# A selective-scan stage in which GpSimd weighs two neighbouring state tiles per operation

## The reference, cut to what matters

```
xc, z = split(x @ in_w.T);  xc = silu(conv(xc));  dt, B, C = split(xc @ x_w.T);  dt = softplus(...)
h[t, d, s] = exp(dt * A[d, s]) * h[t-1, d, s] + dt * B[t, s] * xc[t, d]      # 16 states s
y[t, d]    = sum over s of h[t, d, s] * C[t, s]  +  xc[t, d] * D[d]
out        = (y * silu(z)) @ out_w.T
```

## Time and profile before

| | before |
|---|---|
| median of three runs | 966.7 us |
| the profiled execution's own time | 964.93 us |
| its span | 963.1 us |
| TensorE matmul busy | 790.4 us, 82% of the span |
| VectorE busy | 704.1 us, 73% |
| GpSimd busy | 515.5 us, 54% |
| ScalarE busy | 369.9 us, 38% |

### The profile page before, as it was taken

One profiled execution on the slowest core, in us unless ns is written; L12 is line 12 of the kernel. 1 busy time (PEld: TensorE's weight loads), 2 busy tenths in 40 slices (PEclk: granted clock), 3 DMA queues, 4 the chain that ended last, 5 costly groups with the idle time before them and its releaser, 6 DMA issues. The chain is left out here.

```text
span 963.1 us, 18898 instructions
## 1 busy us (share of the span) xinstructions
PE 790.4 (82%) x7645; PEld 487.0 (51%) x7657; DVE 704.1 (73%) x911; ACT 369.9 (38%) x557; POOL 515.5 (54%) x403
## 2 busy tenths in 40 slices
PE   8888888889998757878877887878887887788696
PEld 4555554556664534545554555545554545455464
DVE  4985985550004018999999999999999898975798
ACT  1220002123333575455555555455655454321000
POOL 5000000000000018999999999999999998970043
PEclk9999998999998977999999999999999998899688
DMA  4000000000000134666676667666666666510001
GB/s 145 4 5 5 4 5 1 1 0 1 1 0 2 50 112 137 194 193 190 192 213 197 189 187 215 196 193 191 191 210 199 174 194 199 175 47 1 0 0 50
DMA packets 55352, 102.68 MB, mean 107 GB/s; under 512 B 11200, under 2 KB 12352, under 8 KB 55264
## 3 DMA queue, kind: packets, MB, share of 16 engines
q1 hardware_dynamic: 55072, 100.74, 34.4%
q0 software_dynamic: 192, 0.72, 0.2%
HBM read 97.87 MB, written 3.54 MB: 105 GB/s over the span
## 5 line engine op out<-in xcount | busy, mean ns | idle before, releaser
L495 POOL TENSOR_TENSOR ring<-ring,big 128x576 f32<-128x576 f32 x206 | 284.8, 1403 | 18.1 <-DVE ring L865 11.8
L179 PE MATMUL banks<-ring,main_params 128*128 128x288 f32 x824 | 248.6, 432 | 4.6 <-POOL ring L495 2.8
L865 DVE TENSOR_TENSOR_SCAN ring<-big,banks 128x576 f32<-128x576 f32 x154 | 202.6, 1340 | 2.3
L179 PEld LDWEIGHTS banks<-ring,main_params 128*128 128x128 f32 x824 | 149.4, 196 | 61.6 <-POOL ring L495 15.3
L853 DVE TENSOR_TENSOR banks<-banks,big 128x576 f32<-128x576 f32 x192 | 143.0, 745 | 29.9 <-PE banks L1173 27.5
L472 POOL COPY big<-normed 128x576 f32<-128x576 f32 x4 | 2.7, 666 | 297.9 <-DVE normed L372 297.9
L672 ACT ACTIVATE big<-big,small 128x576 f32<-128x576 f32 x192 | 142.2, 764 | 27.3 <-DVE ring L865 21.5
L1172 PE MATMUL banks<-big,selectors 96*128 96x512 bf16 x192 | 74.8, 391 | 77.7 <-DVE ring L865 36.7
L979 PE MATMUL banks<-big 32*32 32x288 f32 x3968 | 102.3, 422 | 19.0 <-issue 15.6
L672 ACT ACTIVATE banks<-big,small 128x576 f32<-128x576 f32 x64 | 47.4, 741 | 112.6 <-DVE ring L865 89.8
L979 PEld LDWEIGHTS banks<-big 32*32 32x32 f32 x3968 | 62.4, 103 | 53.8 <-issue 33.8
(11 more groups left out here) (170 smaller groups left out, 1068.2 us busy)
## 6 DMA issues: line engine op xcount, KB each, us to landing
big<-bc_rows SPq DMA_DIRECT2D x640, 144.0 KB, 3.1
bc_rows<-big SPq DMA_DIRECT2D x16, 144.0 KB, 2.4
residual<-x_in SPq DMA_DIRECT2D x4, 288.0 KB, 7.7
out<-big SPq DMA_DIRECT2D x2, 512.0 KB, 3.1
main_params<-main_in SPq DMA_DIRECT2D x1, 895.0 KB, 9.8
big<-front_in POOLq DMA_DIRECT2D x1, 574.5 KB, 7.7
experts<-experts_in SPq DMA_DIRECT2D x1, 512.0 KB, 10.5
main_params<-main_in SPq DMA_DIRECT2D x1, 158.0 KB, 2.8
```

Source lines behind the costliest of these rows:

```text
L179: last = nc.tensor.matmul(PS[rows, 2 * p + a, 0:HALF], lhsT, rhs[:, bass.ds(at + a * HALF, HALF)], start=start, stop=stop, skip_group_chec ...
L495: nc.gpsimd.tensor_tensor(slot, slot, CT[n % 10], ALU.mult).then_inc(weighted, 1)
L865: nc.vector.tensor_tensor_scan(slot, DECAY[m % 3], place, 0.0, ALU.mult, ALU.add).then_inc(scanned, 1)
```

## The change

The ten C buffers and the ten slots become five pairs of 1152 columns. GpSimd's `weigh(k)` multiplies a pair of slots by a pair of C tiles in one operation of 128 x 1152; it waits for the scan of the second tile, and is done at even iterations. Two states of C come in one DMA per direction. TensorE waits for `weighted` of the pair, and its adds are done one tile later: the list ADDS is new. VectorE's `gate_image` moves from tile 3 to tile 4 of the next image.

```diff
-        CT = [big(L) for _ in range(10)]
+        CT = [big(2 * L) for _ in range(5)]
-        SLOT = [RING[:, i * L:(i + 1) * L] for i in range(8)] + MORE
+        SLOT_PAIR = [RING[:, 2 * i * L:2 * (i + 1) * L] for i in range(4)] + [MORE]
+        SLOT = [t[:, i * L:(i + 1) * L] for t in SLOT_PAIR for i in range(2)]
...
-            def spread_row(dst, b, w, s, loaded):
+            def spread_rows(dst, b, w, s, count, loaded):
                 for d in range(2):
-                    sp.dma_start(dst[d * DI:(d + 1) * DI, :],
-                                 BCD[b, w, d, s].unsqueeze(0).to_broadcast([DI, L])).then_inc(loaded, 16)
+                    rows = BCD[b, w, d, s:s + count].rearrange("s t -> (s t)")
+                    sp.dma_start(dst[d * DI:(d + 1) * DI, :], rows.unsqueeze(0).to_broadcast([DI, count * L])).then_inc(loaded, 16)
...
-                if n >= 10:
-                    sp.wait_ge(weighted, n - 9)
-                spread_row(CT[n % 10], b, 1, s, c_loaded[n % 10])
+                if s % 2 == 0:
+                    k = n // 2
+                    if k >= 5:
+                        sp.wait_ge(weighted, k - 4)
+                    spread_rows(CT[k % 5], b, 1, s, 2, c_loaded[k % 5])
...
-            def weigh(n):
-                pool.wait_ge(scanned, n + 1)
-                pool.wait_ge(c_loaded[n % 10], 32 * (n // 10 + 1))
-                slot = SLOT[n % SLOTS]
-                nc.gpsimd.tensor_tensor(slot, slot, CT[n % 10], ALU.mult).then_inc(weighted, 1)
+            def weigh(k):
+                pool.wait_ge(scanned, 2 * k + 2)
+                pool.wait_ge(c_loaded[k % 5], 32 * (k // 5 + 1))
+                slots = SLOT_PAIR[k % 5]
+                nc.gpsimd.tensor_tensor(slots, slots, CT[k % 5], ALU.mult).then_inc(weighted, 1)
...
-                if n >= 1:
-                    weigh(n - 1)
+                if n >= 2 and n % 2 == 0:
+                    weigh(n // 2 - 1)
...
-                if n >= DS and n % DS == 3:
+                if n >= DS and n % DS == 4:
                     gate_image(n // DS - 1)
...
-                pe.wait_ge(weighted, n + 1)
+                pe.wait_ge(weighted, n // 2 + 1)
...
-            ADDS = [[-3], [-2], [-1], [], [0], [1, 2]] + [[s - 3] for s in range(6, DS)]
-            for n in range(-AHEAD, NTILES + 3):
+            ADDS = [[-4], [-3], [-2], [-1], [], [], [0, 1], [2, 3]] + [[s - 4] for s in range(8, DS)]
+            for n in range(-AHEAD, NTILES + 4):
```

More of the change, by code:

```diff
@@ L132, in build_program @@
         TMP = [big(L) for _ in range(2)]
-        MORE = [big(L) for _ in range(2)]
+        MORE = big(2 * L)
         pos[0] = 0
@@ L214, in build_program @@
         rows_stored = [sem(f"rows_stored{i}") for i in range(3)]
-        c_loaded = [sem(f"c_loaded{i}") for i in range(10)]
+        c_loaded = [sem(f"c_loaded{i}") for i in range(5)]
         b_loaded = [sem(f"b_loaded{i}") for i in range(3)]
@@ L441, in _ @@
                         sp.wait_ge(u_pool, m - 2)
-                    spread_row(BT[m % 3], b, 0, s, b_loaded[m % 3])
+                    spread_rows(BT[m % 3], b, 0, s, 1, b_loaded[m % 3])
                 if s == DS - 1 and b + PREPARED < B:
```

## The result

The changed kernel takes 1011.7 us (median of 4, 1008.8 to 1014.3) against 966.3 before: 1.047 times the time, interval 1.044 to 1.050. Forecast were 1011 and slower. The profiled execution took 1014.3 us with a span of 1012.5.

The account below looks back on a forecast made before the run. TensorE's program order, making VectorE wait at L853, was taken as the bound. Order 14.8, two other images 1.6, tail 2.2, clock 33.0, minus 7.3 for old falls: +44.3 us, forecast 1011 us, its own range 1000 to 1021, wider range 984 to 1025.

Parts of the forecast that it names:

- GpSimd: Weighing in pairs: 2616 ns for twice 1403, saving 1.5 us per image, worth nothing unless VectorE waits for it.
- the 0.28 us wait of L860: VectorE's wait for GpSimd's inputs (L489) at tile 15 goes: gain 0.28 us per image.
- The pair's lateness: TensorE's add waiting for the pair: 2.62 us needed of 3.86, so 1.2 left and no cost.
- The order: TensorE's later adds delay bc_rows and input 12 by 1.34 us; net of 0.28 gained, +1.06 per image, +14.8 over 14.
- Rival 1: TensorE's clock holds at 1.00, so only 18.6 us are lost: 985 us, chance 0.18.
- The clock: TensorE's gap ahead of spread 8 halves its clock in nearly every image: 2.2 us each, +33.0 over fifteen.
- the old falls: Clock falls already in the kernel before's time, four waits at L853: minus 7.3 us.
- The tail: End of the scan stage: the last gate waits longer, for a pair's weighing and two adds: +2.2 us.
- DMA: Half as many C loads of twice the size still land in time: zero cost.
- Rival 2: TensorE's clock stays low for longer, over 3.0 us per image: 1025 us, chance 0.10.
- Rival 3: GpSimd is the pace, at the weighing L495, so the kernel gets faster: 955 us, chance 0.05.
- Rival 4: GpSimd's 1152-column operation costs more than two of 576: 1037 us or more, chance 0.03.

Follow-up runs that it names:

- e8: Kernel before with e7's add list and late first C loads, GpSimd weighing single tiles and C one state per DMA: 956.9 us.
- e7: Changed kernel with gate at tile 3, first C load held until the last z, and no add between bc_rows and take_high: 943.9 us.
- e2: Changed kernel with the old add list and the gate back at tile 3, pairs and double loads kept: 983.3 us.
- e3: Changed kernel with 18 and 12 idle matmuls filling TensorE's gap ahead of tile 8 of each image: 978.3 us.
- e1: Kernel before with only the new add list and the gate one tile later, single tiles and single loads kept: 1009.1 us.
- e5: Kernel before with 20 idle matmuls ahead of bc_rows in its own PSUM place: 986.7 us.
- e4: Changed kernel with the gate back at tile 3 and adds spread evenly, tile s - 4 at each iteration from 4 on: 963.6 us.

## Why the prediction was right, point by point

- GpSimd: the pair measured 2627 ns for 2616, and the 0.28 us wait of L860 is gone in the trace. Its speed alone gave nothing, as said; e8 against e7 shows where it would.
- The pair's lateness, priced at nothing: right in the changed order (no wait of VectorE from it), wrong as an argument. I had named the step sizes queued on GpSimd but not put them into the sum; in the old order they make VectorE wait 0.63 us per image (e2).
- The order: e3 isolates it. 31.90 us per image against 31.94 worked out. Rival 1 was priced wrong: with the clock at 1.00 the 7.3 us of the old falls go too, so 966.7 + 18.6 - 7.3 = 978.0 and not 985; e3 took 978.3.
- The clock: 2.2 us per image taken from two falls; 34.13 - 31.90 = 2.23 measured. e1 and e3 show both halves: the order makes the fall without pairs, and filling the gap takes it away. That there is a fall in each of the fifteen images was reasoned; that it costs 2.2 was a pick between 1.7 and 3.0, and its fit is partly luck. A fall has no one price: it lengthens an image by 1.7 us in e5, by 1.2 to 2.9 in e2. The kernel before had two more falls than the prediction looked at, in its last images, after TensorE had been busy 2.19 and 1.45 of 4.00 us, with waits of 0.95 and 1.51:

```profile
820.60:824.60 4.00, 2.19 (x9) 1.00 0.00 0
824.60:828.00 3.40, 3.28 (x9) 0.51 0.76 214
834.30:838.30 4.00, 1.45 (x7) 1.00 0.64 218
838.30:841.70 3.40, 2.94 (x6) 0.50 0.67 207
```

- The stage as a whole. The 7.3 us of falls before, taken off, was a fair booking: the stage of the profiled execution, from the scaling of A (before L847, after L851) to the last gate, grew by 42.8 us (913.40 - 363.54 against 863.97 - 356.93); 44.3 were forecast. By parts: up to input 12 of image 0 it grew by 1.6 us (1.1 in the sum), over the next 13 images by 41.4 (40.6), and from there to the last gate it shrank by 0.2 (+2.7 in the sum).
- The tail: the last gate waits 5.21 us for 3.84, +1.4 in place of +2.2.
- DMA, priced at zero: this step failed, by a size that the range covered. I asked only whether the C tiles come in time, and they do. The ten double loads at the start come with stops of TensorE instead. In the profiled execution the stretch from the last copy of the layer norm (303.65 and 306.38) to the scaling of A grew from 53.3 to 57.2 us, 3.9. It takes 55.6 to 57.9 us in the four traces with double loads at that time and 51.6 to 54.2 in the eight others, so part of the 3.9 is variation.
- That 1011 was met within 1 us owes something to luck. The sum was made for the profiled execution: 1009.2, and that took 1014.3; the median of the four lies 2.6 below it. The last images and the tail were priced 2.9 too high, and 6.6 us ahead of the stage were missing (the 3.9, and 2.7 still earlier).
- Rival 1 (clock holds) describes e3, not the change. Rival 2 (over 3.0 us per image for the clock) did not come: 2.2. Rival 3 (GpSimd is the pace) fell; it becomes true only in e8. Rival 4 fell with the 2627 ns.

What stays open: why e5 and e2 had falls of the clock in about half of their images, what TensorE waits for in its stops at the start, and how much of the other 2.7 us ahead of the scan stage, in code that is the same, comes back in each execution.

## What to carry to other kernels

Of a software-pipelined loop, write down for each engine when each of its instructions can start, not only how much it has to do: here two engines were full and the third, at 80%, set the time through the order in its queue. When adds are moved later, spread them over the iterations; a gap followed by a dense run cost twice here, for the run delayed what was queued behind it (1.0 us per image) and TensorE did most of it at half clock (2.2 us). Before a DMA is made larger, ask what else runs while the loads fill the DMA engines, also outside the stage that they are for.

## What the runs showed of the hardware that I had not expected

TensorE stood still, waiting for nothing that the profile names, while loads filled the DMA engines or just after. Rows of the changed kernel: TensorE's two stops ahead of the scan stage, and the queues in the stretch from 340 to 350 us (packets, MB, share of 16 engines; then KB each and us to landing), and the two stops themselves (length, PE busy, clock, DMA share, GB/s):

```profile
344.77 0.46 PE L1120 MATMUL banks<-big,conv_weights 32*64 32x288 f32 x3 [1.90 <-issue]
...
353.43 0.75 PE L1130 MATMUL banks<-big,main_params 32*64 32x288 f32 x3 [1.40 <-issue]
```

```profile
q1 hardware_dynamic: 794, 2.34, 103.2%
q8 instruction: 1, 0.02, 0.8%
...
big<-bc_rows SPq DMA_DIRECT2D x4, 288.0 KB, 9.5
```

```profile
342.90:344.80 1.90, 0.03 (x5) 1.00 1.03 223
352.00:353.40 1.40, 0.04 (x5) 0.98 0.00 0
```

From 340 to 350 us all 16 DMA engines are full with q1, and a load takes 9.5 us to land where 4.4 is the median. The first stop lies in this stretch (DMA share 1.03). The second comes after the loads have ended (0.00), and so do the stops of 1.1 us in e2 and e3; so full engines are not what all of the stops have in common. The four kernels with double loads at the old time (the changed one, e2, e3, e4) have such stops, 1.1 to 3.3 us in all; the eight other traces have none. That TensorE waited for its next block of instructions, held up behind the loads, is my reading; no run shows it. The Trainium skill, Runtime: NRT & Kernel Launch, "Instruction fetch mechanics", calls the cost of fetching the next block mostly hidden. If the stops are such fetches, these traces disagree with it for double loads at this time.

The other is the regularity of the clock. Once TensorE's gap had come in, the falls came at the same place in each image of the changed kernel and of e1. The distances of images started at 34.43 and 34.30 us and settled at 34.13 to 34.15 in both, though nothing in the program is 34.13 us long, and though e1 weighs tile by tile and the changed kernel in pairs. No run tells why.
